# A two-layer graph attention kernel: head 7's tail regrouped, one weight rounding and one residual moved

## The chip, the cores and the metric

The kernel runs on one core of a Trainium2 chip. The metric is the device time of one execution in microseconds (us). The engines are named as the profile names them: PE (TensorE matmul), PEld (its weight load), DVE (VectorE), ACT (ScalarE), POOL (GpSimd) and SP (SyncE, which issues every DMA here).

## What is computed

Two graph attention layers on 512 nodes, then a residual and a layer norm. Layer 1 has 8 heads of width 768, layer 2 has one.

```python
def gat_layer(x, W, a_s, a_d, b, edge_index, concat):
    h = (x @ W).reshape(n, H, C)
    alpha_s = einsum('nhc,hc->nh', h, a_s); alpha_d = einsum('nhc,hc->nh', h, a_d)
    e = leaky_relu(alpha_s[src] + alpha_d[dst], 0.2)
    e = exp(e - segment_max(e, dst)[dst])
    alpha = e / (segment_sum(e, dst)[dst] + 1e-16)
    return segment_sum(h[src] * alpha[:, :, None], dst).reshape(n, H * C) + b
h = elu(gat_layer(x, W1, a_src1, a_dst1, b1, edges, True))     # 8 heads
x = layernorm(x + gat_layer(h, W2, a_src2, a_dst2, b2, edges, True))
```

## The kernel before

The edges are first counted into a dense 512 x 512 matrix CT, and from then on everything is dense, in float32. A float32 product is made of three fp32r products: each operand is split into a rounded high part (h) and the rest (l), and the kernel adds high x high, low x high and high x low. ACT writes the high parts, DVE or POOL subtract to get the low parts.

Each head h of layer 1 runs in stages, and each stage has its line in the PE program, in this order:

- **B** (L1066, `half_B`): h = x W1, in 8 half tiles (4 node tiles of 128 rows, 2 halves of 384 columns), evicted by ACT into `h32`; ACT writes `hh`, DVE the row sums with the two attention vectors (`asd`, L681) and `hl` (L706).
- **C of the head before** (L1159, `stage_C`): out += g W2 over six blocks c of 128 rows of W2. A block is three passes p (W2h with gh, W2l with gh, W2h with gl) of eight matmuls each (four with 256 and four with 512 columns), all at L1181. Four banks of high and low W2 rows are in use (N2 = 4), so ACT's `high_w2` for block k waits for the block four before it in C, and POOL's `low_w2` (L1010) follows.
- Into C, `sources` and `targets` put transposes (L1098) that spread the attention terms over the partitions; DVE's `maxima` (L726 to L736) stands between them and gives `r12`. `denominators` (L1115, matmuls at L1121 and L1123) sums the exponentials: it needs `gh[:, 0]` of ACT's `high_sums` (L463) and `gl[:, 0]` of DVE (L866), and DVE's reciprocal (L767) needs its result. The caller passes it as `between`, which `stage_C` calls ahead of pass 2.
- **A** (L1141, `stage_A`): P^T h for each c of six (matmuls L1148, L1151, L1154, twelve per c). DVE scales it with the reciprocal (`scale_A`, L779, into `y_row`), ACT takes the exponential, DVE finishes the ELU (`elu`, L785 and L787), ACT writes `gh`, DVE `gl` (`low_g`, L791). A uses the two PSUM banks R0 and R1 in turn: A of c can start when `scale_A` has read c-2 (for c = 3, when it has read c = 1).

Head 7 is the last. Its y of blocks 0 to 2 has a buffer of its own (`y3`); otherwise y goes into three rows of `L` and `y2`. Ahead of its `scale_A`, DVE runs `part_sums` (L793): for each node tile t four multiply-and-sum reductions (L808) over the unfinished output in PSUM with layer 2's attention vectors. Tiles 0 and 1 stand ahead of c = 0, tiles 2 and 3 ahead of c = 1. What head 7 adds to those terms comes from `last_terms` (L1265): for each c and each of four node tiles a plain float32 matmul with the 128 x 128 piece of y as weights and two columns of `va` (W2's rows times layer 2's attention vectors, L700) as moving data, 24 in all, in two groups, after C(7,0) and after C(7,1). DVE adds both into `asd` (L932); then follow `sources`, `maxima`, `targets` and the scores of layer 2.

The end is **D** (L1287): P^T h for layer 2 in four output tiles d, each in a wide (512) and a narrow (256) piece. Tiles 0 and 1 run interleaved over t = 0 to 3; then `tail_denominators` (L1309, four float32 matmuls at L1313), then tiles 2 and 3. DVE turns the denominators into `dn` (L948, L950), and for each d runs `residual` (L963), `stats` (L969), `bn_aggr` (L982), a reciprocal (L986) and a scale (L989) with ACT's square root (L631) between them, and the normalisation: ACT's for d = 0 to 2 (L634), DVE's own for d = 3 (L996). Each output tile is then stored.

Every engine runs its program in the order in which it is written; nothing is reordered but the weight loads of PE. POOL's program is, per head, six `low_w2`, four `low_P` (L1014) and six `low_w1`.

## Time and profile before

| | |
|---|---|
| median of 3 runs | 655.41 us (654.6 to 659.33) |
| profiled execution: time | 655.43 us |
| profiled execution: span, first to last instruction | 653.6 us |
| granted TensorE clock, mean | 0.998 of full speed |
| PE busy | 636.7 us, 97% of the span |
| DVE busy | 510.9 us, 78% |
| ACT busy | 333.3 us, 51% |
| POOL busy | 210.5 us, 32% |
| chain that ended last, by engine | PE 79%, DVE 17%, ACT 2%, issue 1% |

The span runs from the first to the last instruction; the time of an execution is 1.83 us more. The chain that ended last is followed back from the last instruction to whatever released each step, so its shares say which engine set the end. In a timeline, "C(6,4)" below means stage C of head 6, block 4, and rows give start, length, engine, line, operation and count, with idle time before it in brackets.

### The profile page before, as it was taken

The numbers are of one execution on the slowest core, as the hardware profiler recorded it, in microseconds if no ns is written. First come the engines' busy times: TensorE is split into PE (matmuls) and PEld (weight loads), VectorE is DVE, ScalarE is ACT, GpSimd is POOL, SyncE is SP. The second block draws the span as 40 slices with busy tenths as digits, with TensorE's granted clock in tenths as the row PEclk, the third lists the DMA queues.
The fourth block names the chain that finished last, engine by engine and source line by source line (L and its number), as shares of the span: only waits on it lengthen the run. The fifth ranks groups of instructions, "written<-read, shape, count | busy, mean of one in ns | idle before, by whom it ended". The sixth has DMA issues, their size and how long they took to land.

```text
span 653.6 us, 9322 instructions
## 1 busy us (share of the span) xinstructions
PE 636.7 (97%) x3437; PEld 548.6 (84%) x3446; DVE 510.9 (78%) x927; ACT 333.3 (51%) x560; POOL 210.5 (32%) x121
## 2 busy tenths in 40 slices
PE   6999999999999999999999999999999999999995
PEld 4766568989878879988898889988998899878984
DVE  8999996798989977385856684677886687889566
ACT  6799981546614554454445344454436344524272
POOL 0000000140743640357125822473156514551130
PEclk9999999999999999999999999999999999999999
DMA  8422420115143520134113320325043403500002
GB/s 308 161 73 73 157 87 25 49 53 190 49 145 115 176 73 1 49 97 146 49 49 94 108 90 25 97 55 163 25 118 125 131 17 126 210 25 1 2 1 97
DMA packets 22173, 59.36 MB, mean 91 GB/s; under 512 B 2544, under 2 KB 2800, under 8 KB 22128
## 3 DMA queue, kind: packets, MB, share of 16 engines
q1 hardware_dynamic: 22128, 58.76, 27.6%
q8 instruction: 28, 0.46, 0.3%
q14 instruction: 17, 0.14, 0.1%
HBM read 54.03 MB, written 4.72 MB: 90 GB/s over the span
## 4 chain that ended last, share of the span: by engine, by line
PE 79%; DVE 17%; ACT 2%; issue 1%; DMA 0%; SPq 0%; DVEq 0%; ACTq 0%
PE O L1181 21%; PE R L1076 9%; PE R L1082 9%; PE R L1079 9%; PE O L1093 6%; PE R L1148 5%; PE R L1154 5%; PE R L1151 5%; DVE ohd L645 2%; DVE L L752 1%; DVE hl L706 1%; DVE junk L808 1%; PE R L1098 1%; DVE ohs L647 1%; DVE junk L681 1%
## 5 line engine op out<-in xcount | busy, mean ns | idle before, releaser
L1010 POOL TENSOR_TENSOR W2l<-Wr,W2h 128x768 fp32r<-128x768 f32 x48 | 99.1, 2070 | 211.4 <-ACT W2h L404 211.4
L1014 POOL TENSOR_TENSOR Pl<-L,Ph 128x512 fp32r<-128x512 f32 x34 | 53.9, 1595 | 170.6 <-ACT Ph L453 170.3
L1076 PE MATMUL R<-W1h,xTh 128*128 128x384 f32 x312 | 106.6, 342 | 0.0
L1079 PE MATMUL R<-W1l,xTh 128*128 128x384 f32 x312 | 105.5, 338 | 0.0
L1082 PE MATMUL R<-W1h,xTl 128*128 128x384 f32 x312 | 105.5, 338 | 0.0
L681 DVE CUSTOM_DVE_ANT_0 junk<-h,abc 128x768 bf16<-128x768 f32 x64 | 64.6, 1009 | 49.1 <-ACT h L416 47.6
L1181 PE MATMUL O<-W2h,gh 128*128 128x256 f32 (+1 forms) x384 | 78.6, 340 | 0.0
L1181 PE MATMUL O<-W2l,gh 128*128 128x256 f32 (+1 forms) x384 | 77.1, 336 | 0.0
L1181 PE MATMUL O<-W2h,gl 128*128 128x256 f32 (+1 forms) x384 | 77.1, 336 | 0.0
L416 ACT COPY h<-R 128x384 f32<-128x384 f32 x62 | 29.4, 476 | 82.9 <-PE R L1082 74.1
L1148 PE MATMUL R<-Ph,hh 128*128 128x512 f32 x168 | 65.8, 392 | 2.6 <-DVE rb L767 1.8
L1004 POOL TENSOR_TENSOR W1l<-Wr,W1h 128x768 fp32r<-128x768 f32 x30 | 56.1, 1889 | 36.3 <-ACT W1h L393 36.3
L1093 PE MATMUL O<-ohd,ohs 128*128 128x512 bf16 x255 | 60.9, 388 | 5.5 <-DVE ohs L647 4.9
L1154 PE MATMUL R<-Ph,hl 128*128 128x512 f32 x168 | 66.1, 394 | 0.0
L1151 PE MATMUL R<-Pl,hh 128*128 128x512 f32 x168 | 65.9, 392 | 0.0
L1181 PEld LDWEIGHTS O<-W2l,gh 128*128 128x128 f32 x384 | 59.0, 188 | 8.2
L1181 PEld LDWEIGHTS O<-W2h,gl 128*128 128x128 f32 x384 | 58.9, 188 | 8.1
L1181 PEld LDWEIGHTS O<-W2h,gh 128*128 128x128 f32 x384 | 58.1, 188 | 6.6
L404 ACT CAST W2h<-Wr 128x768 fp32r<-128x768 f32 x48 | 39.7, 833 | 42.0 <-PE O L1181 42.0
L1076 PEld LDWEIGHTS R<-W1h,xTh 128*128 128x128 f32 x312 | 58.6, 188 | 1.0 <-ACT h L416 0.2
L1079 PEld LDWEIGHTS R<-W1l,xTh 128*128 128x128 f32 x312 | 58.6, 188 | 0.4
L1082 PEld LDWEIGHTS R<-W1h,xTl 128*128 128x128 f32 x312 | 58.5, 188 | 0.0
(172 smaller groups left out, 1158.6 us busy)
## 6 DMA issues: line engine op xcount, KB each, us to landing
Wr<-in_W SPq DMA_DIRECT2D x101, 384.0 KB, 3.2
abc<-in_as SPq DMA_DIRECT2D x9, 384.0 KB, 4.2
abc<-in_ad SPq DMA_DIRECT2D x9, 384.0 KB, 5.8
h_rows<-h SPq DMA_DIRECT2D x8, 384.0 KB, 2.3
hl<-h_rows SPq DMA_DIRECT2D x8, 384.0 KB, 5.2
xin<-in_xT SPq DMA_DIRECT2D x6, 256.0 KB, 6.0
xr<-in_x SPq DMA_DIRECT2D x1, 1536.0 KB, 6.8
out<-res SPq DMA_DIRECT2D x4, 384.0 KB, 2.3
```

The costliest lines, as they stand in the source:

```text
L681: e.tensor_tensor_reduce(out=junk[:, :], in0=get, in1=a_ap[:, i, :], op0=ALU.mult, op1=ALU.add, scale=1.0, scalar=0.0, accum_out=asd[:, h ...
L1004: e.tensor_tensor(W1l[:, k, :], Wr[:, n, :], W1h[:, k, :].bitcast(f32), ALU.subtract).then_inc(s_w1l, 1)
L1010: e.tensor_tensor(W2l[:, m % N2, :], Wr[:, n, :], W2h[:, m % N2, :].bitcast(f32), ALU.subtract).then_inc(s_w2l, 1)
L1014: e.tensor_tensor(Pl[:, t, d0:d1], L[:, t, d0:d1], Ph[:, t, d0:d1].bitcast(f32), ALU.subtract).then_inc(s_Pl, 1)
L1076: e.matmul(bank[:, 0:HALF], xTh[:, f, xs], hi[:, ws], start=f == 0, stop=False)
L1079: e.matmul(bank[:, 0:HALF], xTh[:, f, xs], lo[:, ws], start=False, stop=False)
L1082: m = e.matmul(bank[:, 0:HALF], xTl[:, f, xs], hi[:, ws], start=False, stop=f == FT - 1)
L1093: e.matmul(O[2 * (g % 2) + q][:, :], ohs[:, r, 128 * q:128 * q + 128], ohd[:, r, :], start=j == STARTS[g], stop=j == STARTS[g + 1] - 1).th ...
L1148: e.matmul(bank[:, :], hh[:, t, cs], Ph[:, t, :], start=t == 0, stop=False)
L1151: e.matmul(bank[:, :], hh[:, t, cs], Pl[:, t, :], start=False, stop=False)
L1154: m = e.matmul(bank[:, :], hl[:, t, cs], Ph[:, t, :], start=False, stop=t == NT - 1)
L1181: mm = e.matmul(ob, ga[:, c, 128 * t:128 * t + 128], wa[:, q, lo:hi], start=first and (hi - lo == 512 or t % 2 == 0), stop=last, skip_grou ...
```

## The change

Six edits, all but one at head 7 or behind it:

1. **`denominators` of head 7** go from block 4 to block 5 of C(6), and there ahead of pass 1 in place of pass 2 (`at=1`): sixteen matmuls later in PE's order.
2. **`part_sums`**: tiles 0 and 1 ahead of c = 0 as before, tile 2 ahead of c = 1, tile 3 ahead of c = 2.
3. **`y3` is gone**: head 7's y uses the three rows that the other heads use.
4. **`last_terms`** has the roles turned: the weights are four columns `vhl` (high and low of `va`, by one small ACT copy and one small DVE subtraction), the moving data are the 512 columns of `gh`, then of `gl` (two weight columns): twelve fp32r matmuls. The second six stand inside C(7,1), ahead of its pass 2. ACT copies the result, 4 x 512, to SBUF (`alr`), and four float32 matmuls (`turned_terms`, weights `alr`, moving `sel`, a 4 x 2 matrix) turn it and add high and low, after C(7,1). The PSUM ring gets one more entry, ("at", 8, 0).
5. **`tail_denominators`** goes ahead of the last t of D's tiles 0 and 1. On DVE, **`residual(3, 0)`** goes ahead of the reciprocal of d = 2.
6. **W2's fourth block, heads 3 to 7**: ACT's `high_w2(h - 1, 3)` and `scaled_as` (which waits for the head's last `asd`) change places.

```diff
-    RING += [("al", H, 0), ("as", H, 0), ("r2", H, 0), ("r1", H, 0), ("tail", 0, 0)]
+    RING += [("al", H, 0), ("at", H, 0), ("as", H, 0), ("r2", H, 0), ("r1", H, 0), ("tail", 0, 0)]
...
+        vhl = sb("vhl", [128, FT, 4], f32r)
+        sel = sb("sel", [4, 2], f32)
...
-        y3 = sb("y3", [128, 3, N], f32, c2)
+        alr = sb("alr", [4, N], f32, c2)
...
+                    scaled_as(h, 8 * h + 8)
                     high_w2(h - 1, NT - 1)
-                    scaled_as(h, 8 * h + 8)
...
                     if h == H - 1:
+                        e.wait_ge(s_v, 2 * FT)
+                        e.copy(vhl[:, :, 0:2], va[:, :, :]).then_inc(s_vh, 1)
                         for k in range(3):
                             high_w2(h, k)
...
             high_w2(H - 1, 4)
+            e.wait_ge(s_al, 1)
+            e.copy(alr[:, :], ring_bank("al", H, 0)[0:4, :]).then_inc(s_ar, 1)
             high_w2(H - 1, 5)
...
+            def low_v():
+                e.wait_ge(s_vh, 1)
+                e.tensor_tensor(vhl[:, :, 2:4], va[:, :, :], vhl[:, :, 0:2].bitcast(f32), ALU.subtract).then_inc(s_vl, 1)
...
                     sums_P(h)
+                    if h == H - 1:
+                        low_v()
...
                 for c in range(FT):
+                    if h == H - 1 and c == 0:
+                        part_sums(0)
                     if h == H - 1 and c < 3:
-                        part_sums(2 * c)
-                        part_sums(2 * c + 1)
+                        part_sums(c + 1)
                     scale_A(h, c)
...
                 if d < 2:
                     residual(d + 1, 1)
+                if d == 2:
+                    residual(3, 0)
                 e.wait_ge(s_rs, 2 * d + 1)
                 e.reciprocal(rs[:, d, 1:2], rs[:, d, 0:1]).then_inc(s_nm, 1)
...
                     if d == 2:
-                        residual(3, 0)
                         stats(3, 0)
...
-                    stage_C(h - 1, c, between=(lambda h=h: denominators(h)) if c == (FT - 2 if h == H - 1 else FT - 1) else None)
+                    stage_C(h - 1, c, between=(lambda h=h: denominators(h)) if c == FT - 1 else None,
+                            at=1 if h == H - 1 else 2)
...
                 bank = take("al", H, 0) if cs[0] == 0 else ring_bank("al", H, 0)
-                e.wait_ge(s_v, 12)
+                e.wait_ge(s_vl, 1)
                 for c in cs:
-                    e.wait_ge(s_g, FT * (H - 1) + c + 1)
-                    for t in range(NT):
-                        m = e.matmul(bank[:, 2 * t:2 * t + 2], y_row(H - 1, c)[:, 128 * t:128 * t + 128], va[:, c, :],
-                                     start=c == 0 and t == 0, stop=c == FT - 1, skip_group_check=True)
+                    e.wait_ge(s_gh, FT * (H - 1) + c + 1)
+                    m = e.matmul(bank[0:4, :], vhl[:, c, :], gh[:, c, :], start=c == 0, stop=c == FT - 1, skip_group_check=True)
+                    e.wait_ge(*gl_value(H - 1, c))
+                    m = e.matmul(bank[0:2, :], vhl[:, c, 0:2], gl[:, c, :], start=False, stop=c == FT - 1, skip_group_check=True)
+                if cs[-1] == FT - 1:
                     m.then_inc(s_al, 1)
+
+            def turned_terms():
+                bank = take("at", H, 0)
+                e.wait_ge(s_sel, 1)
+                e.wait_ge(s_ar, 1)
+                for t in range(NT):
+                    m = e.matmul(bank[:, 2 * t:2 * t + 2], alr[:, 128 * t:128 * t + 128], sel[:, :],
+                                 start=t == 0, stop=True, skip_group_check=True)
+                m.then_inc(s_at, 1)
 
             stage_C(H - 1, 0)
             last_terms((0, 1, 2))
-            stage_C(H - 1, 1)
-            last_terms((3, 4, 5))
+            stage_C(H - 1, 1, between=lambda: last_terms((3, 4, 5)))
+            turned_terms()
             stage_C(H - 1, 2, between=lambda: sources(H, 8 * H + 1))
...
             for t in range(NT):
+                if t == NT - 1:
+                    tail_denominators()
                 for d in range(2):
                     for i in range(2):
                         stage_D(d, t, i)
-            tail_denominators()
```

PE's order around the denominators of head 7, in C(6,4) and C(6,5), before (each row is a run of equal matmuls; a pass is four rows):

```order
2177 L1181 MATMUL O<-W2l,gh 128x256 x2
2178 L1181 MATMUL O<-W2l,gh 128x512 x2
2179 L1121 MATMUL R<-gh,oner 128x512
2180 L1123 MATMUL R<-gl,oner 128x512
2181 L1181 MATMUL O<-W2h,gl 128x256 x2
2182 L1181 MATMUL O<-W2h,gl 128x512 x2
```

and now:

```order
2185 L1193 MATMUL O<-W2h,gh 128x256 x2
2186 L1193 MATMUL O<-W2h,gh 128x512 x2
2187 L1133 MATMUL R<-gh,oner 128x512
2188 L1135 MATMUL R<-gl,oner 128x512
2189 L1193 MATMUL O<-W2l,gh 128x256 x2
```

The two matmuls moved behind pass 2 of C(6,4) and pass 0 of C(6,5).

PE's order in head 7 from the end of C(7,1)'s pass 1 on, now (`vhl` is the split `va`, `alr` ACT's copy of the 4 x 512 result); before, twelve L1272 rows stood behind C(7,1) and none inside it:

```order
2294 L1193 MATMUL O<-W2l,gh 128x512 x2
2295 L1285 MATMUL R<-gh,vhl 4x512
2296 L1287 MATMUL R<-gl,vhl 2x512
2297 L1285 MATMUL R<-gh,vhl 4x512
2298 L1287 MATMUL R<-gl,vhl 2x512
2299 L1285 MATMUL R<-gh,vhl 4x512
2300 L1287 MATMUL R<-gl,vhl 2x512
2301 L1193 MATMUL O<-W2h,gl 128x256 x2
2302 L1193 MATMUL O<-W2h,gl 128x512 x2
2303 L1193 MATMUL O<-W2h,gl 128x256 x2
2304 L1193 MATMUL O<-W2h,gl 128x512 x2
2305 L1297 MATMUL R<-sel,alr 128x2 x4
```

Six wide matmuls now stand ahead of pass 2, which gives ACT that pass's time for its copy, and four small ones behind it.

DVE's order in head 7 from the first scaled row of A on, now (L784 is `scale_A`, L790 and L792 are `elu`, L814 the reductions of `part_sums`, each with a row for its accumulator):

```order
753 L784 TENSOR_TENSOR L<-R,rb 128x512
754 L790 TENSOR_SCALAR L<-L 128x512
755 L792 SCALAR_TENSOR_TENSOR L<-L,b1s 128x512
756 L814 ISA junk,prt<-O,abc 128x512
757 L814 ISA prt 128x1
758 L814 ISA junk,prt<-O,abc 128x512
759 L814 ISA prt 128x1
760 L814 ISA junk,prt<-O,abc 128x256
761 L814 ISA prt 128x1
762 L814 ISA junk,prt<-O,abc 128x256
763 L814 ISA prt 128x1
764 L784 TENSOR_TENSOR y<-R,rb 128x512
```

Before, these four reductions stood ahead of row 753; now they stand behind the ELU of c = 0 and ahead of `scale_A` of c = 2.

## Rows read from the trace of the kernel before

**Rows 1.** Windows: stretch, length, then busy us of PE, PEld, DVE, ACT, POOL.
```profile
475.00:540.00 65.00, 65.00 (x355) 58.77 (x354) 48.65 (x75) 30.23 (x48) 30.57 (x16) 1.00 0.33 102
```
**Rows 2.** Timeline of PE, C(6,4) pass 1, second denominator matmul, start of A(7,0).
```profile
570.81 1.55 PE L1181 MATMUL O<-W2l,gh 128*128 128x256 f32 x8
...
573.45 0.50 PE L1123 MATMUL R<-gl,oner 128*128 128x512 f32 x1 [0.49 <-DVE gl L866]
...
579.35 0.39 PE L1148 MATMUL R<-Ph,hh 128*128 128x512 f32 x1
```
**Rows 3.** Timeline of DVE, head 7: reciprocal, first reduction, scale c = 1, ELU, scale c = 2.
```profile
573.99 3.36 DVE L767 RECIPROCAL rb<-R 128x512 f32<-128x512 f32 x1 [0.59 <-PE R L1123]
579.54 0.69 DVE L808 CUSTOM_DVE_ANT_0 junk<-O,abc 128x512 bf16<-128x512 f32 x1 [2.20 <-PE O L1181]
...
587.79 0.69 DVE L779 TENSOR_TENSOR y<-R,rb 128x512 f32<-128x512 f32 x1
588.39 0.42 DVE L785 TENSOR_SCALAR L<-L 128x512 f32<-128x512 f32 x1
...
589.52 0.68 DVE L779 TENSOR_TENSOR y<-R,rb 128x512 f32<-128x512 f32 x1
```
**Rows 4.** Timeline of PE, start of A(7,3) and of C(7,0).
```profile
588.53 0.50 PE L1148 MATMUL R<-Ph,hh 128*128 128x512 f32 x1 [0.77 <-DVE y L779]
...
596.88 1.55 PE L1181 MATMUL O<-W2h,gh 128*128 128x256 f32 x8
```
**Rows 5.** Timeline of DVE, an ELU's first instruction in head 5.
```profile
450.45 2.08 DVE L785 TENSOR_SCALAR L<-L 128x512 f32<-128x512 f32 x1
```
**Rows 6.** Timeline of POOL, beside that ELU, and W2's block 3 of head 7.
```profile
450.39 1.85 POOL L1004 TENSOR_TENSOR W1l<-Wr,W1h 128x768 fp32r<-128x768 f32 x1 [2.54 <-ACT W1h L393]
...
585.62 1.86 POOL L1010 TENSOR_TENSOR W2l<-Wr,W2h 128x768 fp32r<-128x768 f32 x1 [6.91 <-ACT W2h L404]
```
**Rows 7.** Timeline of PE, first group of last terms and what follows.
```profile
601.05 2.73 PE L1272 MATMUL R<-va,y 128*128 128x2 f32 x24
...
603.65 1.65 PE L1181 MATMUL O<-W2h,gh 128*128 128x256 f32 x8
```
**Rows 8.** Timeline of PE, the denominators of head 6 and what follows.
```profile
507.64 0.40 PE L1121 MATMUL R<-gh,oner 128*128 128x512 f32 x1
...
508.12 1.54 PE L1181 MATMUL O<-W2h,gl 128*128 128x256 f32 x8
```
**Rows 9.** Timeline of PE in D: t = 3, tail denominators, D(2,0), last of D(3,0).
```profile
634.89 0.39 PE L1299 MATMUL O<-hh,Ph 128*128 128x512 f32 x1
...
636.98 0.95 PE L1313 MATMUL R<-oner,y 128*128 128x2 f32 x8
637.79 0.48 PE L1299 MATMUL O<-hh,Ph 128*128 128x512 f32 x1
...
644.64 0.39 PE L1305 MATMUL O<-hh,Pl 128*128 128x512 f32 x1
```
**Rows 10.** Timeline of DVE: last sum of exponentials, residual (0,0), reciprocal, residual (3,0), end.
```profile
633.66 0.69 DVE L943 TENSOR_TENSOR y<-y,rb 128x512 f32<-128x512 f32 x1
...
638.47 0.75 DVE L963 SCALAR_TENSOR_TENSOR res<-O,dn,xr 128x512 f32<-128x512 f32 x1
...
646.75 0.16 DVE L986 RECIPROCAL rs<-rs 128x1 f32<-128x1 f32 x1 [0.70 <-ACT rs L631]
...
647.07 0.75 DVE L963 SCALAR_TENSOR_TENSOR res<-O,dn,xr 128x512 f32<-128x512 f32 x1
...
650.20 0.68 DVE L996 TENSOR_SCALAR res<-res,mv,rs 128x768 f32<-128x768 f32 x1
```
**Rows 11.** Timelines of DVE, PE and POOL: last of r12, targets of head 7, longest low part.
```profile
559.58 0.16 DVE L736 SCALAR_TENSOR_TENSOR r<-asd,mc 128x4 f32<-128x4 f32 x1
...
560.21 1.04 PE L1098 MATMUL R<-idn,r 128*128 128x128 f32 x8
...
468.36 2.61 POOL L1010 TENSOR_TENSOR W2l<-Wr,W2h 128x768 fp32r<-128x768 f32 x1 [16.12 <-ACT W2h L404]
```

34 lines of the change are left out of this document (17 added, 17 removed).

## The prediction, made before the changed kernel had run

> **What bounds the kernel now.** I read the windows first, to see where PE still idles, then PE's timeline at each edit, and last the timelines of DVE, ACT and POOL for the work that releases it. The windows show that PE is busy for the whole of every stretch from 280 to 560 us; one of them, 65.00 of 65.00, stands for all [rows 1]. So in heads 3 to 6 a faster DVE, ACT or POOL gains nothing: only less PE work would. PE idles in two places of head 7: ahead of the second denominator matmul, where it waits for DVE's low part [rows 2], and ahead of A(7,3), where it waits for DVE to read c = 1 [rows 4]. After that PE is busy up to D, and behind D the end is set by DVE: its tail starts only when the tail denominators, which stand behind both interleaved tiles, are through [rows 9, 10].
>
> **The change part by part.** Times are on the clock of the profiled execution (span 653.6 us, time 655.43 us, 0.02 us above the median of the three runs, so no correction is needed).
>
> *Denominators (edit 1).* Pass 1 of C(6,4) starts at 570.81 [rows 2]. A pass has 3072 columns, six times 512, and twelve matmuls of 512 columns take 2.78 us in stage A (three blocks from 588.53 to 596.88 [rows 4]), so a pass takes 1.39. From 570.81 to 579.35 there are 8.54 us for five passes (6.95) and the two denominator matmuls, which so cost 1.59; in head 6 they take 0.48 (507.64 to 508.12) [rows 8]. Moved two passes on, they start at 570.81 + 3 x 1.39 = 574.98; both inputs are there by 573.45, so nothing waits. A(7,0) then starts at 574.98 + 0.48 + 2.78 = 578.24 in place of 579.35 [rows 2]: **-1.1 us**. The price is a later reciprocal: 0.54 us behind the start of L1123 as now (573.45 to 573.99), so 575.22 + 0.44 = 575.7 without the restart after a wait, and with 3.36 us [rows 3] done at 579.0. The first reduction waits for C(6) to end, 0.19 us behind the start of A (579.35 to 579.54); now both allow 579.1: DVE is 0.45 us earlier than before, and the reciprocal is level with it, with no slack. The tiny `low_v` and the ACT copy ahead of it lie in the time in which DVE waited for the denominators; even if `low_v` is held up by a whole POOL instruction (1.86 us [rows 6]) it is through by 575.3, before the reciprocal's input.
>
> *Reductions (edit 2).* Between 579.54 and 587.79 DVE runs four tiles of reductions and one scaling of 0.61: 1.91 us a tile [rows 3]. PE starts A 0.74 us behind the start of the scaling that frees its bank (587.79 to 588.53), and one c takes 2.78 (588.53 to 596.88 for three) [rows 3, 4]. New schedule: reductions 0 and 1 to 582.9, scaling c = 0, reduction 2, scaling c = 1 at 585.4; A(7,2) is due at 583.8 and A(7,3) at 586.6, both free by then (583.7 and 586.2). So the 0.77 us wait is gone. But reduction 3 now stands ahead of scaling c = 2. DVE's ELU of c = 0 starts at 586.0. Without POOL its two instructions take 1.13 us (588.39 to 589.52 [rows 3]). With POOL beside it the first one waits: in head 5 it took 2.08 us in place of 0.42 and ended 0.29 us behind POOL's instruction (452.53 and 452.24) [rows 5, 6]. Here POOL's low part of W2's block 3 ran from 585.62 [rows 6]; its cast stands behind ACT's exponential of c = 0, which moves with DVE, so it comes at 585.2 and ends at 587.0. The ELU's first half then ends at 587.3 and the second 0.71 later, at 588.0. Reduction 3 ends at 589.9, scaling c = 2 starts, and A(7,4) can start at 590.65 where PE is ready at 586.6 + 2.78 = 589.3: a new wait of 1.3 us. The next scaling is at 592.4, and A(7,5) is due at 593.4, so that is the last. C(7,0) starts at 590.65 + 5.56 = 596.2 in place of 596.88 [rows 4]: **-0.7 us for edits 1 and 2 together**; bounds -1.5 (no contention) and 0.
>
> The Trainium skill, "SBUF — State Buffer", section "Who interferes with whom", says that a VectorE instruction in a 2-port mode, and one with two SBUF inputs, waits for the whole of a GpSimd instruction that holds the shared port pair; [rows 5, 6] agree, by that rule the time is the one above, and a reader who held the ports to be separate would come out 0.8 us lower.
>
> *y3 (edit 3).* Head 7 now has the order of the other heads, where PE never waits [rows 1]; the instructions are the same. Zero.
>
> *Last terms (edit 4).* A group of twelve now takes 601.05 to 603.65, 2.60 us [rows 7]; the second has the same twelve matmuls, so 5.20 in all. New: twelve fp32r matmuls with 512 moving columns. The trace has that form with 128 weight columns: 0.24 each in [rows 8], so 2.88. The four turned ones are of the form of the tail denominators, 636.98 to 637.79, 0.81 [rows 9]. Sum 3.69: **-1.5 us**. The bounds for a matmul of 4 weight columns, which no row shows: not below the 0.23 of the moving columns (-1.6), and not above four times the 0.11 us that a float32 matmul of 128 columns takes (1.04 us busy for eight overlapped ones in [rows 11], which start 0.1 apart), that is 0.44 each, 5.3 + 0.8, +0.9. I take 0.24, because operands and columns are those of [rows 8].
> The Trainium skill, "TensorE: Matmul & The Clock Gate", section "Back-to-back issue gap", has 216 ns for 512 columns at full clock; by it the estimate for the twelve is 2.6 us and the gain 1.8, and no row here has so short a gap.
> Behind what waits: the second group needs the last `gl`, which is there at about 602.4, and PE comes at 604.6; ACT's copy (about 0.6) lies beside pass 2 (1.39); ACT's queue behind it holds only W2's block 5, which waits for the end of C(7,1) anyway. DVE's addition L932 stands behind four additions that end at 607.6, and is needed at 608.3. Cover is thin (0.7) there and nothing is added.
>
> So PE is 0.7 + 1.5 = **2.2 us earlier** from C(7,2) on, and the scores of layer 2, which start from its transposes, move with it.
>
> *Tail (edit 5).* t = 3 starts at 634.89 - 2.2 = 632.7; the tail denominators come there and need DVE's last sum, ready at 634.35 - 2.2 = 632.15 [rows 9, 10]: no wait, with 0.5 to spare. With 0.81 for them, the wide piece of tile 0 is done at 632.7 + 0.8 + 0.85 = 634.3, and residual (0,0) starts there and not at 638.47 [rows 10]: DVE's tail is 4.15 us earlier, but PE's D(2) and D(3) only 2.2. Tile 2 is just in time (needed at 638.7, done at 638.6). Aggregation 2 ends at 646.05 - 4.15 = 641.9 (DVE's idle 0.70 ahead of 646.75), and D(3,0) at 645.03 - 2.2 = 642.8: DVE waits 0.9 for PE. From there residual (3,0), then reciprocal and scale (0.32, 646.75 to 647.07), which now follow it, then the rest: 650.20 - 647.07 = 3.13 [rows 10]. The last instruction starts at 642.8 + 3.13 + 0.32 + 0.05 = 646.3 in place of 650.20: **-3.9 us in all**, 2.2 of PE and 1.7 of DVE's tail, whose distance to D(3,0) falls from 5.17 to 3.5. Without that move the reciprocal would come at 646.75 - 4.15 = 642.6 and residual (3,0) at 642.9, behind it: the end would be 0.2 earlier, so this part of the edit costs 0.2.
>
> *W2's block 3 (edit 6).* Zero where PE is full. The cast moves 1.3 us back, behind the last sum; POOL's low part no longer holds up `hl`. Block 3 is used two blocks of C (8 us) later. What could be lost is the slack of `r12`: it ends at 559.74, and PE needs it at 560.21 [rows 11], 0.47 us.
>
> The sum: 655.4 - 3.9 = **651.5 us**.
>
> **The rivals.**
> - *No contention:* ELU and POOL miss each other (POOL's cast comes later, or DVE gets in first). Then C(7,0) is 1.5 earlier and the end 4.7: 650.7. For it: the margin between the two starts is under 1 us. Against: in head 7 both hang on the same scaling.
> - *Partial:* narrow matmuls cost 0.44, or the sum L943 comes late and PE waits at the tail denominators, or the wait ahead of A(7,4) is 2 us and more. Each takes 0.7 to 2.4 back: 652.2 to 653.9. For it: slack of 0.5 and of zero, above.
> - *The other side, edit 6:* in each of five heads POOL now has two low parts end to end from 555.2 on. At 1.86 each they end at 558.9, ahead of the four small instructions of `r12`, which read two SBUF inputs and would wait for POOL. At the longest, 2.61 [rows 11], they end at 560.4, `r12` at 561.1, and PE waits 0.9 a head, 4.5 in all: 656.0, slower than before. It decides from 0.8 us a head. Against: low parts beside `maxima` took 1.86, and 2.61 needs DVE work with two SBUF inputs beside it.
> - *It does nothing:* the 2.2 us of PE shift are given back in layer 2's scores, where ACT's chain is full. Then only the tail's 1.7 stays: 653.7. Against: that chain starts from PE's transposes and its work is unchanged.
>
> **How the numbers follow.** The forecast (651.0 to 652.1) has 0.45, the first rival 0.2, the partial one 0.2, the last 0.08, edit 6 0.04; 0.03 is left for what I have not seen. The range 650.2 to 653.8 holds all but the edges of these. A measurement here can tell about 1% (6.6 us) from no change. Faster by more needs under 648.9, below every case above: 0.05. Slower by more needs over 662: 0.02.
>
> **What would show each step.** In the new profile: no PE wait at the denominators and A(7,0) at about 578.2; a PE wait of about 1.3 us ahead of A(7,4), with DVE's L785-type row of over 1 us beside a POOL row; twelve matmuls at 0.24; C(7,2) 2.2 earlier; residual (0,0) at about 634.3; DVE waiting 0.9 for D(3,0). Wrong would be: PE waits at the transposes of heads 3 to 7, a wait of PE at the tail denominators, or a narrow matmul of over 0.3.

## The result, and the profile after

The kernel after takes **650.71 us** (median of 6 executions, 649.9 to 651.04) against 655.41 before (6 executions, 654.6 to 659.33). The ratio estimated from all executions is 0.9908, with a 95% interval of 0.9888 to 0.9928; that of the two medians is 0.9928. Forecast were 651.5 and 3.9 us; the medians are 4.7 apart. The profiled execution of the kernel after took 650.08 us with a span of 648.3; that of before had 655.43 and 653.6, so the two profiles are 5.3 apart.

The timeline of TensorE in the kernel after, where [rows 2, 4, 7] stand for before (start, duration, engine, line, operation, out<-in, shapes, count, in brackets the idle time ahead and what ended it):

```profile
569.84 1.54 PE L1193 MATMUL O<-W2l,gh 128*128 128x256 f32 x8
...
573.99 0.40 PE L1133 MATMUL R<-gh,oner 128*128 128x512 f32 x1
574.22 0.40 PE L1135 MATMUL R<-gl,oner 128*128 128x512 f32 x1
...
577.24 0.39 PE L1160 MATMUL R<-Ph,hh 128*128 128x512 f32 x1
...
588.20 0.40 PE L1166 MATMUL R<-Ph,hl 128*128 128x512 f32 x1
589.43 0.50 PE L1160 MATMUL R<-Ph,hh 128*128 128x512 f32 x1 [0.83 <-DVE y L784]
...
595.13 1.54 PE L1193 MATMUL O<-W2h,gh 128*128 128x256 f32 x8
...
599.28 0.40 PE L1285 MATMUL R<-gh,vhl 128*4 128x512 f32 x1
599.51 0.39 PE L1287 MATMUL R<-gl,vhl 128*2 128x512 f32 x1
...
606.32 1.05 PE L1297 MATMUL R<-sel,alr 4*128 4x2 f32 x8
607.30 1.67 PE L1193 MATMUL O<-W2h,gh 128*128 128x256 f32 x8
```

What the prediction said of TensorE in head 7 is there: no wait at the denominators, a new one ahead of A(7,4), and matmuls of four weight columns 0.23 apart. The new wait is 1.0 us (588.20 to 589.43, where neighbours start 0.23 apart), forecast were 1.3. But the first row was not foreseen: pass 1 of C(6,4) starts at 569.84, where it started at 570.81 [rows 2], and **0.97 us is gained before any edited instruction of head 7 runs**.

VectorE at the new wait, and its tail (for [rows 3, 10]), with GpSimd's row beside the first:

```profile
584.20 0.69 DVE L784 TENSOR_TENSOR L<-R,rb 128x512 f32<-128x512 f32 x1
584.80 1.27 DVE L790 TENSOR_SCALAR L<-L 128x512 f32<-128x512 f32 x1
...
586.78 0.68 DVE L814 CUSTOM_DVE_ANT_0 junk<-O,abc 128x512 bf16<-128x512 f32 x1
...
588.69 0.68 DVE L784 TENSOR_TENSOR y<-R,rb 128x512 f32<-128x512 f32 x1
...
633.39 0.75 DVE L974 SCALAR_TENSOR_TENSOR res<-O,dn,xr 128x512 f32<-128x512 f32 x1 [0.40 <-PE O L1330]
...
640.76 0.21 DVE L993 BATCH_NORM_AGGREGATE mv<-st 128x2 f32<-128x12 f32 x1
641.61 0.75 DVE L974 SCALAR_TENSOR_TENSOR res<-O,dn,xr 128x512 f32<-128x512 f32 x1 [0.64 <-PE O L1330]
642.28 0.15 DVE L999 RECIPROCAL rs<-rs 128x1 f32<-128x1 f32 x1
...
644.88 0.68 DVE L1008 TENSOR_SCALAR res<-res,mv,rs 128x768 f32<-128x768 f32 x1
```
```profile
583.94 1.85 POOL L1022 TENSOR_TENSOR W2l<-Wr,W2h 128x768 fp32r<-128x768 f32 x1 [6.12 <-ACT W2h L405]
```

The ELU's first half (L790) took 1.27 us and ended at 586.07, 0.28 behind GpSimd's instruction (585.79): the contention of [rows 5, 6] was forecast for this place. The last instruction starts at 644.88 in place of 650.20 [rows 10].

Where the heads changed is seen where TensorE goes from one stage to the next in heads 5 and 6. Kernel before, first matmul of a stage A, of the next B, C and A:

```profile
440.79 0.39 PE L1148 MATMUL R<-Ph,hh 128*128 128x512 f32 x1
...
457.28 0.34 PE L1076 MATMUL R<-W1h,xTh 128*128 128x384 f32 x1
...
482.72 0.40 PE L1181 MATMUL O<-W2h,gh 128*128 128x256 f32 x2
...
509.50 0.39 PE L1148 MATMUL R<-Ph,hh 128*128 128x512 f32 x1
```

Kernel after, the same four:

```profile
440.22 0.39 PE L1160 MATMUL R<-Ph,hh 128*128 128x512 f32 x1
...
457.02 0.34 PE L1088 MATMUL R<-W1h,xTh 128*128 128x384 f32 x1
...
481.99 0.28 PE L1193 MATMUL O<-W2h,gh 128*128 128x256 f32 x1
...
508.78 0.39 PE L1160 MATMUL R<-Ph,hh 128*128 128x512 f32 x1
```

Stage A takes 16.80 us instead of 16.49 (440.22 to 457.02), B, with nothing in it but 144 matmuls, 24.97 instead of 25.44, and C 26.79 instead of 26.78 here, 26.69 in the other heads. From one head to the next it is 68.45 us instead of 68.71 (68.56 for the head shown). PE is busy all through in both kernels: these are the same matmuls at another pace.

### The profile page after: what moved, and what is told of

Its sections match the earlier page's. It is cut to its first block, busy times and chain, and to the rows that moved or that the text cites. A ratio compares the mean times of both kernels' runs of the same rounds, so it can differ in the third digit from the quotient of the medians.

```text
span 648.3 us, 9280 instructions
## 1 busy us (share of the span) xinstructions
PE 634.2 (98%) x3418; PEld 542.3 (84%) x3418; DVE 514.4 (79%) x929; ACT 333.9 (52%) x562; POOL 207.3 (32%) x121
## 4 chain that ended last, share of the span: by engine, by line
PE 86%; DVE 11%; issue 2%; ACT 1%; DMA 0%; SPq 0%; DVEq 0%; ACTq 0%
PE O L1193 23%; PE R L1088 10%; PE R L1094 10%; PE R L1091 10%; PE O L1105 9%; PE R L1160 5%; PE R L1166 5%; PE R L1163 5%; PE R L1110 1%; DVE hl L711 1%; DVE junk L814 1%; DVE junk L686 1%; DVE rb L772 1%; PE O L1160 1%; PE O L1163 1%
## 5 line engine op out<-in xcount | busy, mean ns | idle before, releaser
L1022 POOL TENSOR_TENSOR W2l<-Wr,W2h 128x768 fp32r<-128x768 f32 x48 | 95.3, 1996 | 212.7 <-ACT W2h L405 212.7
L473 ACT ACTIVATE L<-L,b1s 128x512 f32<-128x512 f32 x32 | 23.2, 724 | 64.3 <-DVE L L784 64.3
```

The costliest lines, as they stand in the source:

```text
L1022: e.tensor_tensor(W2l[:, m % N2, :], Wr[:, n, :], W2h[:, m % N2, :].bitcast(f32), ALU.subtract).then_inc(s_w2l, 1)
```

## The experiments

The question was: what sets that pace, and how much of the result is the edits' own? Each run below is compared with the kernel before on the same chip. The instructions of heads 3 to 6 are the same in both kernels, but for edit 6 in each of them.

### First: is it the execution, or edit 6?

c0_before is the kernel before, c1_after the kernel after. e1_w2_alone is before with edit 6 alone, e2_all_but_w2 is after with it undone:

```diff
-                    high_w2(h - 1, NT - 1)
                     scaled_as(h, 8 * h + 8)
+                    high_w2(h - 1, NT - 1)
```

> The kernel before, unchanged, for its scatter and a second profile. Two theories are at issue. Theory R (rate): the 1.0 us by which the changed kernel was ahead at C(6,4), before any edit of head 7 acts, is a difference of TensorE's pace between two executions, a quarter of a microsecond a head; then this second profile has its own pace, and the distance between the transposes of two heads (68.7 us in the first profile) may come out anywhere from 68.4 to 68.8 with the same program. Theory W (edit 6): the pace of the kernel before is 68.7 us a head and only moving the rounding of W2's fourth row block makes it 68.46; then this profile shows 68.7 again. Ratio 1.000 by both.

> The kernel before with edit 6 alone. Theory W: heads 3 to 7 gain 0.25 us each, 1.2 us in all, ratio 0.998. Theory R: nothing, ratio 1.000 within 0.001, since TensorE never waits in these heads. Both: DVE's last low part of h falls from 2.6 to 0.95 us, and the first small instruction behind the maxima waits for POOL (0.77 us in place of 0.16).

> The changed kernel with edit 6 undone. Theory W: 1.2 us slower than the changed kernel, 3.5 to 4.1 us under the kernel before, ratio 0.9945. Theory R: as the changed kernel within 0.4 us, 4.3 to 5.0 us under the kernel before, ratio 0.993.

> The changed kernel again, on the same chip as the three others. By both theories about 4.7 us under the kernel before, ratio 0.9928; by theory R its head distance in the profile is that of the kernel before on this chip within 0.3 us, by theory W 0.25 shorter.

| run | median us | ratio to before [95%] | from head to head | stages B, C, A |
|---|---|---|---|---|
| c0_before | 657.23 | 1.0019 [1.0002, 1.0035] | 68.72 | 25.44, 26.78, 16.49 |
| e1_w2_alone | 658.04 | 1.0024 [1.0, 1.0049] | 68.72 | 25.44, 26.78, 16.49 |
| e2_all_but_w2 | 652.06 | 0.9939 [0.9923, 0.9956] | 68.45, but 69.6 and 69.5 into heads 6 and 7 | 24.96, 26.69, 16.80; C 27.84 and 27.74 in heads 6 and 7 |
| c1_after | 650.37 | 0.9916 [0.9898, 0.9934] | 68.45 | 24.96, 26.69, 16.80 |

Both theories fell. The pace belongs to the program (a stage's length repeats to 0.01 us from run to run, so it is not the execution), and it does not go with edit 6 (it is in e2 and not in e1). Yet edit 6, which I had put at zero, is worth 1.7 us in the kernel after (650.37 against 652.06) and little in the kernel before: the fastest executions are at 654.9 in e1_w2_alone and at 654.8 in c0_before. Of what both theories expected of e1, the last low part of h did fall from 2.6 to 0.95 us; the small instruction behind the maxima did not wait for GpSimd (0.16 us, not 0.77). Without it TensorE waits at the source transposes; e2_all_but_w2, VectorE with GpSimd and TensorE beside it:

```profile
480.16 2.48 DVE L705 CUSTOM_DVE_ANT_0 junk<-Wr,abc 128x768 bf16<-128x768 f32 x1
...
483.82 2.49 DVE L686 CUSTOM_DVE_ANT_0 junk<-h,abc 128x768 bf16<-128x768 f32 x1
```
```profile
483.58 1.92 POOL L1022 TENSOR_TENSOR W2l<-Wr,W2h 128x768 fp32r<-128x768 f32 x1 [1.75 <-ACT W2h L405]
```
```profile
486.47 0.62 PE L1110 MATMUL R<-idn,asd 128*128 128x128 f32 x4 [0.94 <-DVE asd L686]
```

GpSimd's low part of W2's block 3 starts 0.24 us ahead of VectorE's last sum (483.58 and 483.82), which then takes 2.49 us instead of 0.96. In the kernel before it is the other way round at this place, and the sum pays nothing:

```profile
484.43 0.96 DVE L681 CUSTOM_DVE_ANT_0 junk<-h,abc 128x768 bf16<-128x768 f32 x1
```
```profile
485.08 2.01 POOL L1010 TENSOR_TENSOR W2l<-Wr,W2h 128x768 fp32r<-128x768 f32 x1 [1.55 <-ACT W2h L404]
```

The Trainium skill, "SBUF — State Buffer", section "Who interferes with whom", says that a VectorE instruction with two SBUF inputs contends with a GpSimd instruction that reads SBUF, and the trace agrees, for this custom reduction too (0.96 to 2.49). So the faster stage B turned the order of arrival in heads 6 and 7, where VectorE has the products L705 to do as well; in heads 3 to 5 of e2 GpSimd comes 0.65 us behind the last sum, as in the kernel before, and the sum takes 0.96. Edit 6 puts GpSimd's instruction behind the sums, where its place no longer hangs on a quarter of a microsecond.

A second thing shows in the window of 604 to 607 us, the stretch behind the first group of last terms. Columns as in [rows 1], then the granted clock of TensorE, DMA share and GB/s. Kernel before, c0_before and e1_w2_alone, in this order:

```profile
604.00:607.00 3.00, 3.00 (x20) 2.62 (x19) 3.00 (x3) 0.00 (x0) 0.75 (x1) 1.00 0.00 0
```
```profile
604.00:607.00 3.00, 3.00 (x12) 2.61 (x12) 3.00 (x3) 0.00 (x0) 1.21 (x1) 0.51 0.00 0
```
```profile
604.00:607.00 3.00, 3.00 (x11) 2.61 (x12) 3.00 (x3) 0.00 (x0) 1.00 (x1) 0.50 0.00 0
```

The granted clock was 1.00 (2.4 GHz) in the first and about 0.5 (1.2 GHz) in the other two. It fell at the end of a stretch of 2.7 us in which TensorE ran the first group of last terms, 24 matmul records of two columns; c0_before:

```profile
601.53 2.83 PE L1272 MATMUL R<-va,y 128*128 128x2 f32 x24
604.23 2.91 PE L1181 MATMUL O<-W2h,gh 128*128 128x256 f32 x8
606.94 1.81 PE L1181 MATMUL O<-W2l,gh 128*128 128x256 f32 x8
```

The pass from 604.23 took 2.71 us, a pass at the full clock 1.39. From C(7,0) to C(7,2) c0_before needs 15.19 us (597.37 to 612.56), the first profile of before 13.62 (596.88 to 610.50): 1.57 us for one such fall. e1_w2_alone had two falls, at the first and at the second group of last terms.

The mean granted clock of each execution tells how often it happened. For the kernel before it was 0.998 in the first profile, 0.994 in c0_before's with one fall, and 0.989 in e1_w2_alone's with two. The 23 executions of the kernel before on that chip fall into the same three groups: 15 with 0.997 or 0.998 at 654.4 to 655.9 us, median 655.2; six with 0.994 or 0.995 at 656.6 to 657.8; two with 0.989 at 660.4 and 661.1. No execution of the kernel after is below 0.997, and they lie within 1.2 us. So a median of before can hold a fall, and below the executions are also compared group by group, which leaves the falls out.

### Second: does the place of the tiles in SBUF set the pace?

What was left that touches every head was the allocation. `vhl` (96 bytes) and `sel` (32 with rounding) are allocated ahead of `asd`, and all that comes behind them (W1's halves, L, P's halves, y2, g's halves) moves up by 128 bytes. x's, h's and W2's halves stand ahead and don't move.

m1_pace has TensorE alone:

```python
for k in range(12): m = e.matmul(Q[0][:, 0:512], S[:, 0:128], M[:, 16:528], start=k == 0, stop=k == 11)
...
```

> None of the reference's work is done; TensorE alone runs groups of twelve fp32r matmuls on two SBUF tiles that both begin at a multiple of 1024 bytes, one group a line: first 512 columns with the moving operand's start stepped by 32 bytes from 0 to 992 and the weights at 0, then the same in steps of 64 bytes with the weights at 128, then 384 columns in steps of 32 bytes. Why the question: in the kernel before a matmul of 384 columns (stage B) starts 0.174 to 0.180 us behind the last one and one of 512 (stage A) 0.225 to 0.231, in the kernel after it is 0.173 and 0.230 to 0.236. Theory L (the place of a tile in SBUF sets TensorE's pace; the two new tiles push all that is allocated behind them up by 128 bytes): the distance from one start to the next depends on the moving operand's start by 0.003 to 0.010 us in a pattern that repeats. Rival X (the pace depends on what the other engines do at that moment, not on the place alone): all groups of 512 columns show one distance within 0.001 us, and so do all of 384.

The distances (starts of one line's matmuls, mean without the first) do depend on the place, with a period of 256 bytes: with the weights at 0, lines whose moving start differs by 256 agree to 0.001 us. With 512 columns they run from 0.2267 (moving at 0) over 0.2289 (64) and 0.2333 (32, 128) to 0.2345 (96). With the weights at 128 the shortest stand where the moving operand is at 128 or 384, and there the mean is 0.231 in the first such line and 0.229 in the later ones, of which only the last six distances are 0.227: some of what went before shows in a line's first matmuls. Rival X fell: nothing else ran.

e11_gap is the kernel before and a hole of 128 bytes; e12_after_unshifted is the kernel after with its tiles last of all:

```diff
+        sb("gap", [128, 32], f32)
         asd = sb("asd", [128, 2, 2, NT], f32)
```
```diff
-        vhl = sb("vhl", [128, FT, 4], f32r)
-        sel = sb("sel", [4, 2], f32)
         asd = sb("asd", [128, 2, 2, NT], f32)
...
         gl = sb("gl", [128, FT, N], f32r)
+        vhl = sb("vhl", [128, FT, 4], f32r)
+        sel = sb("sel", [4, 2], f32)
```

> The kernel before with one unused tile of 128 bytes ahead of asd, so that every tile allocated behind it stands where the kernel after has it; no instruction differs. Theory L: the distance from one head to the next falls from 68.71 to 68.45 us (stage B 25.44 to 24.96, stage A 16.49 to 16.80), and since edit 6 is not in it, heads 6 and 7 may lose about 1.1 us each at the sources, as they did when edit 6 was undone in the kernel after; time 653.5 to 657. Rival X (one of the instructions that the diff adds or moves sets the pace): 68.71 as before, PE's matmul of 384 columns at 0.174 to 0.180 us, time as the kernel before within 0.3%.

> The kernel after with its two new tiles allocated last of all, so that every other tile stands where the kernel before has it. Theory L: heads 68.71 us apart again, B 25.44 and A 16.49; the second turn of the head's sums takes 0.96 us and not 2.5; about 1.0 us slower than the kernel after by the four heads' pace: 651.4, less if the first three heads pay nothing. Rival X: heads stay 68.45 apart, 650.4.

| run | median us | ratio to before [95%] | stages B, C, A of an undisturbed head |
|---|---|---|---|
| e11_gap | 657.44 | 1.0019 [0.9999, 1.0039] | 24.96, 26.69, 16.80 |
| e12_after_unshifted | 651.17 | 0.9918 [0.9891, 0.9945] | 25.44, 26.78, 16.49 |

Theory L holds for the stages: with the hole alone, and not one instruction changed, the stages of the kernel after appear, and with the tiles put last they go. e11_gap, TensorE, the same stage starts as above, and its wait at the sources of head 6:

```profile
440.22 0.39 PE L1149 MATMUL R<-Ph,hh 128*128 128x512 f32 x1
...
457.02 0.34 PE L1077 MATMUL R<-W1h,xTh 128*128 128x384 f32 x1
...
481.99 0.28 PE L1182 MATMUL O<-W2h,gh 128*128 128x256 f32 x1
...
487.16 0.62 PE L1099 MATMUL R<-idn,asd 128*128 128x128 f32 x4 [0.87 <-DVE asd L682]
```

The hole by itself makes the kernel slower, which the medians hide (657.44; the kernel before had 657.32 on that chip). Executions with a mean clock of 0.997 or more have a median of 655.15 before (nine) and of 657.2 with the hole (eight), 2.0 us more. In the profiles C takes 0.96 and 1.01 us more in heads 6 and 7 than before, and A(7,0) starts at 580.42 where it started at 579.35: what B brings is more than lost to the sums beside GpSimd. Hole and edit 6 together bring a gain.

e12_after_unshifted is the cleanest test of the prediction's own sum, as nothing outside the edits moves. Its median of 651.17 is 4.0 us below those 655.15 of the kernel before. Against the profile of before, with both counted from the source transposes of head 7 (555.27 here, 555.60 before):

| point | before | e12 | moved | forecast |
|---|---|---|---|---|
| A(7,0) | 579.35 | 577.88 | -1.14 | -1.1 |
| C(7,0) | 596.88 | 595.70 | -0.85 | -0.7 |
| C(7,2) | 610.50 | 607.91 | -2.26 | -2.2 |
| last instruction | 650.20 | 645.80 | -4.07 | -3.9 |

### Third: the edits one by one

e10u_terms is before with edits 4 and 3 (y3 is gone in it too), its two tiles last of all. e4_den_sums has edits 1 and 2 alone, e5_tail_den the move of the tail's denominators alone (their diffs are the corresponding parts of the change).

> The kernel before with edit 4 alone (head 7's last terms with rows as the moving operand, and the turned terms), its tiles allocated last so that no other tile moves. The prediction's step says -1.5 us at C(7,2) and nothing else moved. Theory D (the old last terms let TensorE's granted clock fall in some executions, which costs 1 to 3 us in these): the clock's records show 1.0 from the first matmul of stage C of head 7 to D's start, the time's scatter (before: 654.4 to 661) falls under 1 us, and the median falls by more than 1.5, to about 652.5. Rival (the fall is not bound to the old last terms): scatter as before, median 653.9.

> The kernel before with edits 1 and 2 alone (head 7's denominators one part earlier, one part sum less ahead of A(7,0) and the last one ahead of A(7,2)); no tile moves. The prediction's steps: A(7,0) -1.1 us, C(7,0) -1.8 us, of which 1.3 us is given back ahead of A(7,4) already; so C(7,0) at 595.1 in an execution whose clock holds (before: 596.9), and 653.6 against 655.4. Rival (the place of the tiles brought this too): A(7,0) where it was within 0.2 us.

> The kernel before with the tail's denominators ahead of the last t of stage D; no tile moves. The prediction's step: residual(0, 0) starts 1.7 us earlier against D's first matmul than it did (9.84 us behind it instead of 11.5 or so less the 0.3 of the moved matmuls), and the end moves by about 1.7: a median of 653.7 against 655.4. Rival (the last transfer or the statistics at the end take it back): under 0.5 us.

- **Edit 4, with 3.** Median 654.42, 12 executions between 653.3 and 655.0, ratio 0.9959 [0.9941, 0.9977]. C(7,0) to C(7,2) takes 12.20 us (596.94 to 609.14) instead of 13.62: -1.42, and the profile's clock is 1.00 in this stretch. Of theory D the falls and the scatter came: none of the 12 has a mean clock below 0.996, and the scatter fell from 5.9 to 1.7 us, not quite under 1. Its time did not: 652.5 was expected, and 654.42 is nearer to the rival's 653.9. Against executions of before without a fall (655.15) it is 0.7 us and not 1.4, though the profile alone is 1.3 faster; why the executions gain less stays open. What of the old last terms lets the clock fall, their two columns, their number or their type, was not separated.
- **Edits 1 and 2.** Median 656.58, ratio 1.0015 [0.9995, 1.0035]: no gain to be seen in the time. The profiled execution had one fall of the clock (0.59 in the window of 604 to 607), so it goes beside c0_before: last instruction 651.04 against 652.27, with the source transposes at 555.72 and 556.08, so -0.87. A(7,0) came at 578.33 and C(7,0) at 596.16: counted from the source transposes -1.14 and -0.84. The expectation misread the prediction, whose 0.7 at C(7,0) already includes the 1.1 at A(7,0), and asked for 1.8; by the prediction's step it agrees. All 12 executions have a mean clock of 0.995 or less, so none went without a fall: placed 0.8 us earlier, the old last terms met one every time, and why is open. The nine with 0.995 have a median of 656.44, the six of before on that chip with 0.994 or 0.995 one of 657.8: -1.3.
- **The tail's denominators.** Median 656.1, ratio 0.9992 [0.9968, 1.0017], and again a clock of 0.64 in the window of 604 to 607. The executions stand in three groups by their mean clock: five with 0.999 at 652.6 to 653.6, median 653.4, four with 0.996 at 656.0 to 656.6 and three with 0.991 at 658.6 to 659.0. The 15 of before on that chip with 0.997 or more have a median of 655.5: -2.1. Counted from D's first matmul, which the clock cannot blur, residual (0,0) starts 8.05 us behind (631.22 to 639.27) instead of 9.84, and the last instruction 19.78 instead of 21.57: **-1.79**.

For edits 1 and 2 and for the tail, then, the medians of all executions show nothing, since the falls of the clock are as large as the effects; the profiles and the groups do.

### Fourth: a better place for the tiles

If the place decides, it can be chosen. e13_aligned puts a hole ahead of x's halves and moves `asd`, `amx`, `zm`, `vhl` and `sel`, so that the halves of x, h, W2, P and g all start at a multiple of 256 bytes, and W1's 160 above. e14_aligned_combined also takes away what the new wait ahead of A(7,4) hangs on, and puts residual (3,0) back:

```diff
-                    if h == H - 1 and c == 0:
+                    if h == H - 1 and c == 5:
                         high_w2(h, 3)
```

> The kernel after with its tiles placed otherwise, and no instruction changed: xT's, h's and W2's halves, P's and g's halves all begin at a multiple of 256 bytes, W1's at 160 above one. Theory L (TensorE's distance from one matmul to the next goes by the two operands' starts modulo 256 bytes, as the run on TensorE alone shows: 0.2267 us for 512 columns with both at 0 against 0.2327 with 192 between them): stage A's matmuls at 0.227 instead of 0.2334, so A 16.3 us instead of 16.80; stage C's long ones at 0.227 instead of 0.229, so C 26.5 instead of 26.69; B stays at 24.96; heads 67.8 apart instead of 68.45, and 646 to 648 us in all. Rival (the agreement of the two-tile run with the kernel was chance, other engines' accesses set the pace): stages within 0.1 us of the kernel after, 650.4.

> The run before this one, with head 7's cast of W2's fourth row block moved behind its last exponential (from c = 0 to c = 5) and residual(3, 0) put back where the kernel before has it. Theory S (the wait ahead of A(7,4) has as its last cause an ELU that takes 1.27 us beside POOL's subtraction for that row block, where 0.42 is usual): that ELU takes 0.42 and the wait falls from 1.3 us to about 0.5, the rest being the third part sum's; with 0.2 from the residual, 0.8 to 1.0 us faster than the run before. Rival (POOL's subtraction then meets another of VectorE's operations, or C(7,3) waits for W2's block): within 0.3 us of the run before.

e13: 648.8 us, ratio 0.9889 [0.9866, 0.9912], a little outside the expected 646 to 648. B 24.96 and A 16.33, as expected (16.3), but C 26.88 where 26.5 was expected: its long matmuls went to 0.233 (from 0.229) and not to 0.227. Heads are 68.18 us apart. e14: 647.8, ratio 0.9872 [0.9849, 0.9895]. The wait ahead of A(7,4); e13_aligned, then e14_aligned_combined, TensorE, and VectorE of the latter:

```profile
587.70 0.50 PE L1161 MATMUL R<-Ph,hh 128*128 128x512 f32 x1 [1.12 <-DVE y L785]
```
```profile
586.49 0.50 PE L1160 MATMUL R<-Ph,hh 128*128 128x512 f32 x1 [0.29 <-DVE y L785]
```
```profile
582.73 0.42 DVE L791 TENSOR_SCALAR L<-L 128x512 f32<-128x512 f32 x1
```

From the matmul ahead it was 1.51 us in e13 and is 0.67 in e14, and the ELU takes 0.42. Theory S holds for the wait: 0.84 us of it was GpSimd's instruction beside the ELU. Its 0.2 us for the residual did not come; the tail became 0.13 us longer (below).

What in the places decides C, and whether B and A follow one rule, was open. m2_stages runs the three stages' sequences over a grid of places; e15_g_shifted is e14 with g's halves 192 bytes above a multiple of 256; e16_g_sums3 is that with the last part sum one c later:

```diff
-                    if h == H - 1 and c < 3:
-                        part_sums(c + 1)
+                    if h == H - 1 and c in (0, 1, 3):
+                        part_sums((1, 2, 0, 3)[c])
```

> None of the reference's work is done; behind a warming-up of 60 matmuls TensorE runs short pieces of the sequences of stage A (512 columns, three matmuls with one block of weights), B (384 columns) and C (256, 256, 512, 512 columns), one piece a line, with the weights' tile starting 0, 64, 128 or 192 bytes and the moving one 0 to 224 bytes in steps of 32 above a multiple of 256. Theory L: the kernels' stages are met at their own places: A 0.229 at (weights 128, moving 192), 0.233 at (128, 64), 0.227 at (0, 0); B 0.177 at (128, 160), 0.173 at (128, 32) and (0, 160); C's long ones 0.2305 at (192, 128), 0.229 at (64, 128), 0.233 at (0, 0). Rival: C's places make no difference on an idle chip, and something else in the kernel does.

> The last kernel (e14_aligned_combined) with four small tiles moved ahead of g's halves, so that these begin 192 bytes above a multiple of 256 and W2's at 0 (64 bytes between them, as in the kernel after). Theory L: stage C 26.7 instead of 26.88, with its long matmuls at 0.229 to 0.230 instead of 0.233; A 16.33 and B 24.96 unchanged; the denominators' matmuls, which read g too, within 0.02; 646.6 against 647.8. Rival (C's pace has another cause): C 26.88, 647.8.

> The run before this one with the part sums of tile 3 ahead of scaling c = 3 instead of c = 2. Theory S: PE's distance of 0.67 us ahead of A(7,4) falls to 0.23 and no other wait comes, since the scaling of c = 3 and its sums lie in time in which A(7,5) is not yet due: 0.4 faster than the run before. Rival (the wait goes to A(7,5), or C(7,0) waits for the sums): within 0.2 of the run before.

m2_stages, TensorE, stage A's sequence with the weights' tile at 0 and the moving one at 0, 32, 64 and 96 (L38, L40, L42, L44), then with the weights' tile at 128 and the moving one at 128 and 160:

```profile
26.34 2.88 PE L38 MATMUL Q<-M,S 128*128 128x512 f32 x12
29.06 2.97 PE L40 MATMUL Q<-M,S 128*128 128x512 f32 x12
31.86 2.92 PE L42 MATMUL Q<-M,S 128*128 128x512 f32 x12
34.62 2.97 PE L44 MATMUL Q<-M,S 128*128 128x512 f32 x12
...
82.12 2.89 PE L78 MATMUL Q<-M,S 128*128 128x512 f32 x12
84.84 2.97 PE L80 MATMUL Q<-M,S 128*128 128x512 f32 x12
```

Twelve matmuls take 2.72 us from L38 to L40, 2.80 to L42, 2.76 to L44; and again 2.72 from L78 to L80, where both tiles are at 128. Within this grid the difference of the two starts decides, and the places themselves do not. Over all four places of the weights, the mean distance without a line's first (for C, behind its 512-column matmuls) by that difference (moving less weights, modulo 256 bytes), in us. The four agree to 0.001, but for one of A's (0.2288 at difference 0, the third line behind a change of the weights' place), which is left out:

| difference | 0 | 32 | 64 | 96 | 128 | 160 | 192 | 224 |
|---|---|---|---|---|---|---|---|---|
| A, 512 columns | 0.2267 | 0.2334 | 0.2289 | 0.2346 | 0.2333 | 0.2338 | 0.2328 | 0.2322 |
| B, 384 columns | 0.176 | 0.173 | 0.173 | 0.177 | 0.176 | 0.174 | 0.175 | 0.175 |
| C, its 512 columns | 0.233 | 0.235 | 0.232 | 0.233 | 0.232 | 0.233 | 0.231 | 0.232 |

Held against the kernels (their own mean distances):

| stage | difference before, after, e13 | table | in the kernel |
|---|---|---|---|
| A | 64, 192, 0 | 0.229, 0.233, 0.227 | 0.2291, 0.2334, 0.227 |
| B | 32, 160, 160 | 0.173, 0.174, 0.174 | 0.177, 0.173, 0.173 |
| C, 512 columns | 192, 64, 0 | 0.231, 0.232, 0.233 | 0.231, 0.229, 0.233 |

For stage A the table is met to 0.001 us. For B it is right in the kernel after and in e13 but not in the kernel before, which is slower than its place says, and for C it ranks 0 last, rightly, and the other two the wrong way round: 0.232 at 64, where the kernel has 0.229. A rule for them needs more than this pair of starts (B's weights change from x's high to its low half within a group, which the short sequence leaves out); it stays open.

e15: **647.0 us**, ratio 0.9852 [0.9827, 0.9876]; C is back at 26.69 with the difference of the kernel after (64), though both its tiles stand elsewhere: for this difference the place itself does not matter in the kernel either. A 16.34 and B 24.96 stayed. e16: **646.66 us**, ratio 0.9847 [0.9819, 0.9874], with no wait ahead of A(7,4). Half of it went on to A(7,5), as the rival said, which starts 0.45 us behind the matmul ahead (587.57 to 588.02) where neighbours are 0.23 apart:

```profile
588.02 0.50 PE L1160 MATMUL R<-Ph,hh 128*128 128x512 f32 x1
```

A(7) takes 16.69 us instead of 16.96; the 0.3 us between the medians of e15 and e16 are in the direction of theory S, but at five executions each (646.53 to 647.71 and 646.25 to 647.28) the times alone would not show it. e16 beats both kernels: it is 3.7 us below c1_after's median, on another chip. About 2.3 of that is the place of tiles in heads 3 to 7 (68.45 to 67.99 from head to head, five times) and about 0.6 the same in the first three heads (241.34 us from the first matmul of B(0) to that of B(3), 241.96 in the kernel after); the rest is about the wait (0.8).

## Why the prediction was right, and where it was not

- **The denominators** (-1.1 at A(7,0)): right, -1.14 in e12 and in e4, and between the two profiles once the 0.97 is taken off.
- **The part sums** (-0.7 at C(7,0), with a new wait of 1.3 ahead of A(7,4)): right, -0.85 in e12 and -0.84 in e4. The wait, over the usual 0.23 between two starts, was 1.0 us in the kernel after, 1.2 in e12 and e4 and 1.3 in e13, its place and both its causes as forecast; e14 took one away (0.84), and e16 moved the other from A(7,4) (0.44) to A(7,5) (0.22). "No contention", the rival at 0.2, was wrong about the cause, although its time, 650.7, is the measured one: that is luck.
- **y3** (zero): right for the instructions. But the tiles that edits 3 and 4 take and add were looked at only for what is computed in them.
- **The last terms** (-1.5): right in the profiles, -1.42 in e10u and -1.41 in e12: the turned ones took 0.98 us instead of 0.81 and the twelve with four or two weight columns 0.23 instead of 0.24 each. The undisturbed executions of e10u gained only 0.7. The estimate from the 216 ns of the Trainium skill, "TensorE: Matmul & The Clock Gate", section "Back-to-back issue gap", a gain of 1.8, was too high: the shortest mean distance for 512 columns in any run is 0.227.
- **The tail** (-1.7): right, -1.79 with the denominators alone (e5) and -1.89 with both moves (e12, 19.68 against 21.57). Only its last part was wrong: moving residual (3,0) up was to cost 0.2 us. From D's first matmul to the last instruction it is 19.58 to 19.68 with it moved (after, c1, e2, e12, e13) and 19.78 to 19.83 without (e5, e14, e15, e16), so it gains 0.1 to 0.2. The reciprocal needs ACT's result, which comes 0.9 us behind the start of the aggregation; ScalarE in the kernel after:

```profile
641.36 0.28 ACT L636 ACTIVATE rs<-mv,epc 128x1 f32<-128x1 f32 x1
```

  It ends at 641.64, and D(3,0) is ready just as early: the residual starts at 641.61. The prediction had VectorE wait 0.9 us for D(3,0), longer than the 0.70 for ACT, so that the two small instructions would have fitted in between. The wait was 0.64, so in the old order they would have held the residual up by about 0.3 (638.29 to 638.60 in e15). Behind it they cost less than the 0.37 reckoned: from the residual to the last instruction it is 3.27 us, where it was 3.13.
- **Edit 6** (zero): wrong in the kernel after, right in the kernel before. The step that failed is "Zero where PE is full": PE is full only as long as the sums come in time, and I looked for the slack of `r12` behind them, not at the sums ahead of it. They had a GpSimd instruction starting 0.65 us behind the last one. In the new layout it starts 0.24 ahead and without the edit costs 1.7 us. The rival for this edit, two low parts end to end that hold up `r12`, showed in small: the first of the four instructions (L735) takes 0.94 us in head 6 and 0.77 in head 7 of the kernel after, where 0.16 is usual. The slack covered it but for 0.10 us in head 6 (C 26.79 instead of 26.69).
- **The step that failed most** is one the prediction has no line for: that the unchanged stages of heads 3 to 6 keep their pace ("in heads 3 to 6 [...] only less PE work would" gain). It put this term at nothing without a reason. The allocation changed it by -0.48 + 0.31 - 0.09 = -0.26 us a head. From the first matmul of B(3), with five stages B and four A ahead of C(6,4), that is 1.49 us; less the 0.28 that the same tiles cost in the first three heads and 0.24 by which B(0) began later, it is the 0.97 ahead of C(6,4).
- **The chances**: 0.93 lay on no change that a measurement can tell, and that failed. By the medians the change is 0.7%, but the ratio's interval of 0.9888 to 0.9928 lies wholly below 1: six executions of each tell a difference of well under the "about 1%" that the prediction took for the least that can be told. Most of the scatter of before has a cause, the falling clock, and the change removes it: the six executions of the kernel after lie within 0.2%.

So of 4.7 us by the medians, 3.9 were forecast and are confirmed (4.07 in e12's profile, 4.0 by its executions); the rest, 0.5 to 0.8, is the layout with edit 6 (651.17 without the shift, 650.4 to 650.7 with it). Between the two profiles it is 5.3, and the layout's share 1.2. The first median of before, 655.41, is hardly moved by falls, since undisturbed executions on other chips lie around 655.2 to 655.5; the other four sets of before have medians of 655.4 to 657.8, depending on how many falls they hold, and against those the change looks up to 2 us larger.

## What to carry to other kernels

When a change adds or removes a tile, write down which operands move and by how much, before calling the untouched stages unchanged; here 128 bytes alone made the kernel before 2.0 us slower and, with edit 6, the changed kernel 0.5 to 0.8 us faster. Where an engine is full, ask of each of its suppliers how much later it could come, and whether another order of two instructions on a shared port would use that up. And when the times of the kernel before scatter in steps, read the granted clock of several executions before calling it noise, since a change may remove the cause.

## What the runs showed of the hardware

- The distance between fp32r matmuls of 512 columns depends on the difference between the starts of the moving operand and of the weights modulo 256 bytes: 0.2267 us at 0, 0.2346 at 96, 3.5% more, with nothing else running (m2_stages); the first few behind another line's can be off by up to 0.01. For 384 columns it is 0.173 to 0.177, and there and for C the difference alone does not foretell the kernel's pace.
- At the end of a stretch of about 2.7 us of two-column matmuls the granted clock fell to 1.2 GHz in some executions, at a cost of 1.57 us in c0_before; in e4_den_sums it did so in all 12. With 512 moving columns in their place neither a profile nor one of e10u's 12 executions showed it.
- VectorE's custom reduction over two SBUF operands took 0.96 us, and 2.49 when a GpSimd subtraction of 1.92 us had started 0.24 us ahead of it (e2_all_but_w2); when VectorE came first by 0.65 us it took 0.96 (before).
